# Edge tiles of a graph layer: one three-column product in place of two two-column ones, and one weighting op in place of two

## What is computed

```python
xn = layernorm(x)
Wh = xn @ W_w + W_b
e = (Wh @ a_w[:256])[dst] + (Wh @ a_w[256:])[src] + a_b      # one number per edge
e = where(e > 0, e, 0.2 * e)
ex = exp(e - segment_max(e, src)[src])
gnn = relu(segment_sum(ex[:, None] * Wh[dst], src) / segment_sum(ex, src))
x = x + gnn + linear_attention(xn)                           # 8 heads
x = x + moe(layernorm(x))                                    # 8 experts, top 2, gelu
```

## Time and profile before

| | |
|---|---|
| median of the runs | 2009.92 us (2008.76 to 2011.73) |
| span of the profiled execution, first to last instruction | 2207.5 us |
| instructions in it | 40303 |
| TensorE, matmuls | 78% busy, 13588 |
| VectorE | 76% busy, 4220 |
| ScalarE | 44% busy |
| GpSimd | 45% busy |
| mean granted TensorE clock | 0.895 |

### The profile page before, as it was taken

How to read it: one execution, slowest core, us unless ns; L and a number is a source line. 1 busy time by engine, 2 the same in 40 slices (tenths; PEclk the granted TensorE clock), 3 DMA queues, 4 the chain that set the end, 5 groups by cost and what they waited for, 6 DMA issues and landing times.

```text
span 2207.5 us, 40303 instructions
## 1 busy us (share of the span) xinstructions
PE 1718.1 (78%) x13588; PEld 1259.6 (57%) x13588; DVE 1669.8 (76%) x4220; ACT 976.2 (44%) x2300; POOL 994.8 (45%) x988
## 2 busy tenths in 40 slices
PE   3778785574785688888757888887888888889998
PEld 2557573463674466666535555555555555566666
DVE  5998998663566677776767887888888888886665
ACT  6322221121332233222235656666666656575655
POOL 3000003425566655655666666666666666640000
PEclk7898997796898788888968999999999999999999
DMA  5011111124554444333333333333333333860000
GB/s 174 16 59 52 51 66 32 42 84 115 145 165 130 118 120 119 102 94 90 90 90 87 86 90 83 94 83 94 82 95 92 86 92 83 89 56 11 11 20 13
DMA packets 121460, 182.21 MB, mean 83 GB/s; under 512 B 21490, under 2 KB 91902, under 8 KB 121214
## 3 DMA queue, kind: packets, MB, share of 16 engines
q0 software_dynamic: 45312, 120.06, 23.3%
q1 hardware_dynamic: 75904, 59.25, 8.6%
HBM read 152.43 MB, written 26.63 MB: 81 GB/s over the span
## 4 chain that ended last, share of the span: by engine, by line
DVE 42%; PE 23%; issue 16%; another core or an unknown queue 10%; ACT 4%; DVEq 2%; POOL 1%; DMA 0%; SPq 0%; ACTq 0%; POOLq 0%
PE bank L1255 6%; PE bank L1271 5%; DVE mloc L1615 4%; DVE big L1518 4%; DVE scr L1637 3%; DVE big L1523 3%; DVE work L1809 3%; DVE big L1520 2%; DVE big L1525 2%; DVE big L1796 2%; DVE scr L1483 2%; DVE work L1593 2%; DVE work L1610 2%; PE bank L947 1%
## 5 line engine op out<-in xcount | busy, mean ns | idle before, releaser
L664 POOL DMA_INDIRECT work<-table,tiles x904 | 921.0, 1019 | 546.6 <-PE bank L1142 277.8
L1271 PE MATMUL bank<-big 128*128 128x256 f16 x2352 | 327.7, 278 | 34.8 <-issue 34.5
L1255 PE MATMUL bank<-scr,big 128*128 128x512 f16 (+1 forms) x1248 | 282.3, 377 | 0.3 <-ACT big L871 0.3
L1140 PE MATMUL bank<-work,scr 128*128 128x257 f16 x904 | 269.9, 299 | 13.0 <-issue 10.5
L1271 PEld LDWEIGHTS bank<-big 128*128 128x128 f16 x2352 | 232.3, 99 | 78.3 <-issue 46.0
L1141 PE MATMUL bank<-work,scr 128*128 128x256 f16 x904 | 270.8, 300 | 5.9 <-issue 5.6
L1142 PE MATMUL bank<-work,scr 128*128 128x257 f16 x904 | 268.9, 297 | 5.9 <-issue 5.9
L1637 DVE SCALAR_TENSOR_TENSOR scr<-scr,gg,bank 128x257 f32<-128x257 f32 x452 | 216.7, 479 | 29.7 <-remote 16.6
L999 PE MATMUL bank<-big 128*128 128x208 f16 x1568 | 176.9, 269 | 67.7 <-DVE big L1525 60.9
L799 ACT ACTIVATE work<-bank 128x1024 f16<-128x1024 f16 x113 | 115.5, 1022 | 242.7 <-DVE mloc L1615 144.0
L999 PEld LDWEIGHTS bank<-big 128*128 128x128 f16 x1568 | 150.7, 102 | 94.6 <-issue 88.9
(11 more groups left out here) (340 smaller groups left out, 3494.1 us busy)
## 6 DMA issues: line engine op xcount, KB each, us to landing
work<-table,tiles POOLq DMA_INDIRECT x904
scr<-normed_cols SPq DMA_DIRECT2D x98, 128.0 KB
table<-big SPq DMA_DIRECT2D x49, 129.0 KB, 2.1
normed_rows<-scr SPq DMA_DIRECT2D x49, 128.5 KB, 2.6
big<-normed_rows SPq DMA_DIRECT2D x49, 128.5 KB
normed_cols<-big SPq DMA_DIRECT2D x49, 128.0 KB, 1.7
xs<-in_x_dram SPq DMA_DIRECT2D x4, 1536.0 KB, 14.2
out_dram<-work SPq DMA_DIRECT2D x48, 128.0 KB
```

What stands on the lines that cost most here:

```text
L664: pool.indirect_dma_start(G[:, r, j, :], None, table, bass.IndirectOffsetOnAxis(ap=col[:, t:t + 1], axis=0)).then_inc(rows_in[r // GS], 16)
L1140: pe.matmul(of[:, 0:D + 1], hi, Gh[:, r, j, 0:D + 1], start=(j == 0), stop=False)
L1255: mm = pe.matmul(bank[5 + f][:, 0:n * P], w1p[pw][:, e, h, f * P:(f + 1) * P], x2p[b % 2][px][:, h, 0:n * P], start=(h + m == 0), stop=(h ...
L1271: mm = pe.matmul(of, hTp[ph][:, k % 2, f, (j + c) * P:(j + c + 1) * P], w2p[pw][:, e, f, :], start=False, stop=(f == 1 and m == 2))
```

## The change

It does four things:

1. `prA` and `prB` become one tile `rowp` with four float16 columns per group: row value, its rest, maximum, and one unused column. `spread` makes one product of three columns per tile into a PSUM tile with three columns, where it made two of two columns.
2. `edge_scores` gets a new first op: a sum over the first two of the three columns (`tensor_reduce` from PSUM into the new tile `s0`), with a hand-over to the op that was the first.
3. `w4h` and `w4l` become halves of one tile, and one `tensor_tensor` of 2048 elements writes both weighted one-hots; it waits for `w4l`.
4. `frg` has `coff` subtracted once ahead of the loop, so that the op for `cc` adds two tensors and needs no pointer scalar. The memset of `prB` (L1560) goes.

```diff
-        prA = tiles[:, place_t:place_t + NG + 1].bitcast(F16).rearrange("p (g c) -> p g c", c=2)
-        prB = tiles[:, place_t + NG + 1:place_t + 2 * NG + 2].bitcast(F16).rearrange("p (g c) -> p g c", c=2)
+        rowp = tiles[:, place_t:place_t + 2 * NG + 2].bitcast(F16).rearrange("p (g c) -> p g c", c=4)
...
-        Shi = [piece(NC // 2, P, 2, dt=F16) for _ in range(2)]
-        Slo = [piece(NC // 2, P, 2, dt=F16) for _ in range(2)]
+        S = [piece(2, NC // 2, P, 2, dt=F16) for _ in range(2)]
...
-        w4h = sb("w4h", [P, ST], F16)
-        w4l = sb("w4l", [P, ST], F16)
+        w4p = sb("w4p", [P, 2 * ST], F16)
+        w4h, w4l = (w4p[:, k * ST:(k + 1) * ST] for k in range(2))
...
-            return bank[2][:, 0:2 * ST].rearrange("p (j c) -> p j c", c=2)
+            return bank[2][:, 0:3 * ST].rearrange("p (j c) -> p j c", c=3)
...
-                    of = spread_of(s)[:, j, :]
-                    pe.matmul(of, OT[:, j, :], prA[:, g + 1, :], start=True, stop=False)
-                    mm = pe.matmul(of, OT[:, j, :], prB[:, g + 1, :], start=False, stop=True)
+                    mm = pe.matmul(spread_of(s)[:, j, :], OT[:, j, :], rowp[:, g + 1, 0:3], start=True, stop=True)
...
-            link(dve.memset(prB[:, :, :], 0.0))
-            link(dve.memset(prA[:, 0:1, :], 0.0))
+            link(dve.memset(rowp[:, 0:1, :], 0.0))
...
-            dve.tensor_tensor(prB[:, 1:NG + 1, 0], frg, prA[:, 1:NG + 1, 0], ALU.subtract).then_inc(fr_parts, 1)
+            dve.tensor_tensor(rowp[:, 1:NG + 1, 1], frg, rowp[:, 1:NG + 1, 0], ALU.subtract).then_inc(fr_parts, 1)
+            dve.wait_ge(fr_parts, 1)
+            link(dve.tensor_scalar(frg, frg, coff[:, :], None, ALU.subtract))
...
+                dve.tensor_reduce(s0[:, :], spread_of(s)[:, :, 0:2], AX.X, ALU.add).then_inc(e_s0, 1)
+                dve.wait_ge(e_s0, s + 1)
                 dve.tensor_tensor(s1[:, :].rearrange("p (r j) -> p r j", r=GS),
-                                  spread_of(s)[:, :, 0].rearrange("p (r j) -> p r j", r=GS),
+                                  s0[:, :].rearrange("p (r j) -> p r j", r=GS),
                                   G[:, r:r + GS, :, D + 1], ALU.add).then_inc(e_s1, 1)
...
-                dve.tensor_tensor(s3[:, :], s2[:, :], spread_of(s)[:, :, 1], ALU.subtract).then_inc(e_s3, 1)
+                dve.tensor_tensor(s3[:, :], s2[:, :], spread_of(s)[:, :, 2], ALU.subtract).then_inc(e_s3, 1)
...
-                dve.tensor_tensor(w4l[:, :], w4[:, :], w4h[:, :], ALU.subtract).then_inc(e_w4l, 1)
+                dve.tensor_tensor(w4l, w4[:, :], w4h, ALU.subtract).then_inc(e_w4l, 1)
                 if s > 1:
                     dve.wait_ge(e_A, GS * (s - 1))
-                dve.tensor_tensor(Shi[s % 2], hot[s % 2], pairs(w4h[:, :], P, 1), ALU.mult)
                 dve.wait_ge(e_w4l, s + 1)
-                dve.tensor_tensor(Slo[s % 2], hot[s % 2], pairs(w4l[:, :], P, 1), ALU.mult).then_inc(e_S, 1)
+                a = w4p[:, :].rearrange("p (i r u) -> p i r u", r=1, u=2).to_broadcast([P, NC, P, 2])
+                dve.tensor_tensor(S[s % 2].rearrange("p k i r u -> p (k i) r u"),
+                                  hot[s % 2].rearrange("p (k i) r u -> p k (i r u)", k=1).to_broadcast([P, 2, NC * P]),
+                                  a, ALU.mult).then_inc(e_S, 1)
...
-                dve.scalar_tensor_tensor(cc[:, :], mx[:, k, 1:GS + 1], coff[:, :], frg[:, g:g + GS], ALU.subtract, ALU.add
-                                         ).then_inc(e_cc, 1)
+                dve.tensor_tensor(cc[:, :], mx[:, k, 1:GS + 1], frg[:, g:g + GS], ALU.add).then_inc(e_cc, 1)
```

More of the change, by code:

```diff
@@ L333, in graph_layer @@
         gg = sb("gg", [P, 4, GS])
+        s0 = sb("s0", [P, ST])
         s1 = sb("s1", [P, ST])
@@ L349, in graph_layer @@
         bank = [ctx.enter_context(nc.psum_tensor(f"bank{n}", [P, 512], F32)) for n in range(8)]
-        loaded = {n: sem("loaded_" + n) for n in ("edges", "neighbours", "x", "raw", "weights", "experts0", "experts1", "b2", "list")}
+        loaded = {n: sem("loaded_" + n) for n in ("edges", "neighbours", "raw", "weights", "experts0", "experts1", "b2", "list")}
         filled, padded = sem("filled"), sem("padded")
@@ L382, in graph_layer @@
         rows_in = [sem(f"rows_in{i}") for i in range(GR // GS)]
-        (e_fdp, e_hot, e_V, e_VT, e_ml, e_mx, e_cc, e_R, e_dR, e_gg, e_OT, e_EX, e_s1, e_s2,
+        (e_fdp, e_hot, e_V, e_VT, e_ml, e_mx, e_cc, e_R, e_dR, e_gg, e_OT, e_EX, e_s0, e_s1, e_s2,
          e_s3, e_w4, e_w4l, e_S, e_A, e_U) = (sem("e_" + k) for k in (
-             "fdp", "hot", "V", "VT", "ml", "mx", "cc", "R", "dR", "gg", "OT", "EX", "s1", "s2",
+             "fdp", "hot", "V", "VT", "ml", "mx", "cc", "R", "dR", "gg", "OT", "EX", "s0", "s1", "s2",
              "s3", "w4", "w4l", "S", "A", "U"))
@@ L771, in _ @@
             act.activation(frg, bank[0][:, 0:NG], ACT.Identity, bias=abb[:, :])
-            act.activation(prA[:, 1:NG + 1, 0], bank[0][:, 0:NG], ACT.Identity, bias=abb[:, :]).then_inc(meta_sb, 1)
+            act.activation(rowp[:, 1:NG + 1, 0], bank[0][:, 0:NG], ACT.Identity, bias=abb[:, :]).then_inc(meta_sb, 1)
             for p in range(FIRST_EARLY, EARLY):
@@ L782, in exps @@
                 act.activation(w4[:, :], s3[:, :], ACT.Exp)
-                act.activation(w4h[:, :], s3[:, :], ACT.Exp).then_inc(e_w4, 1)
+                act.activation(w4h, s3[:, :], ACT.Exp).then_inc(e_w4, 1)
             def values(s):
@@ L1138, in total @@
                     n = g % GS * GT + j
-                    hi, lo = (S[s % 2][:, n // 2, :, n % 2] for S in (Shi, Slo))
+                    hi, lo = (S[s % 2][:, k, n // 2, :, n % 2] for k in range(2))
                     pe.matmul(of[:, 0:D + 1], hi, Gh[:, r, j, 0:D + 1], start=(j == 0), stop=False)
@@ L1620, in shifts @@
                 dve.wait_ge(e_mx, s + 1)
-                dve.scalar_tensor_tensor(cc[:, :], mx[:, k, 1:GS + 1], coff[:, :], frg[:, g:g + GS], ALU.subtract, ALU.add
-                                         ).then_inc(e_cc, 1)
+                dve.tensor_tensor(cc[:, :], mx[:, k, 1:GS + 1], frg[:, g:g + GS], ALU.add).then_inc(e_cc, 1)
                 dve.wait_ge(e_cc, s + 1)
-                dve.scalar_tensor_tensor(prA[:, g + 1:g + GS + 1, 1], cc[:, :], ALPHA, cc[:, :], ALU.mult, ALU.max
+                dve.scalar_tensor_tensor(rowp[:, g + 1:g + GS + 1, 2], cc[:, :], ALPHA, cc[:, :], ALU.mult, ALU.max
                                          ).then_inc(e_R, 1)
@@ L1628, in shifts @@
                     dve.wait_ge(e_gg, s - 1)
-                dve.tensor_tensor(dR[:, s % 2, :], prA[:, g:g + GS, 1], prA[:, g + 1:g + GS + 1, 1], ALU.subtract
+                dve.tensor_tensor(dR[:, s % 2, :], rowp[:, g:g + GS, 2], rowp[:, g + 1:g + GS + 1, 2], ALU.subtract
                                   ).then_inc(e_dR, 1)
```

## The result

The changed kernel takes 2026.38 us (2024.89 to 2027.71) against 2009.34 us: the ratio is 1.0085, with a 95% interval of 1.0071 to 1.0099, so 17 us slower (14 to 20). Forecast were +10.1 us and 2020.0.

The account below looks back on a forecast made before the run. VectorE was taken to set most steps of the loop's second half, the first half only in part. Terms 14.0 + 4.4 - 3.9 - 4.4 gave +10.1 us, so 2009.9 became 2020.0 us; the 8-in-10 range was 1997 to 2036.

Parts of the forecast that it names:

- The sign and its cause: Whole loop: slower by 10.1 us, as VectorE sets most steps of the second half; chance of slower 0.56.
- s0: VectorE's new sum ahead of L1582: 0.165 us plus 0.035 hand-over, 0.20 a step, +14.0 us.
- 70 of 113 steps: L1582's pieces in the chain of waits, taken as the steps that pay for the new sum; the other 43 hide it.
- The weighting op: Single op of 2048 elements on VectorE: 1.33 to 1.34 us against 1.28, +0.055 a step, x 80, +4.4 us.
- w4l must be done first (0.20 as above): Ahead of the single weighting op: it starts 0.20 us after the w4l op, the next op 1.13 later.
- cc: VectorE's op without pointer scalar: 225 ns become 0.16 to 0.17 us, -0.055 a step, x 71, -3.9 us.
- TensorE: Spread products: 8 of 16 go, third column free, -0.2 us a step in 22 steps of the chain, -4.4 us.
- The span: Profiled 2207.5 us, to become 2217.6; runs supposed to lack many unnamed waits, terms carried over unscaled to 2009.9 us.
- (a): Loop: the added work is hidden, GpSimd's gathers set the first half's pace; 2014 us or less, to 2006; chance 0.20.
- (b): TensorE's instruction fetch: 7.4 packets fewer save 16 to 36 us; at 3 us each, 1998 us; chance 0.24.
- (c): Single weighting op loses its two-at-a-time rate, 2.29 us instead of 1.22, +86 us, 2108 us; chance 0.04.

Follow-up runs that it names:

- the second sum: The changed kernel with the sum s0 made twice, the second time after a wait for the first: 2047.80 us, ratio 1.0180.
- the doubled add: The kernel before with L1582, the first op of edge_scores, and its hand-over made twice: 2031.87 us, ratio 1.0098.
- the new profile: The kernel before, unchanged, measured and profiled once more: 2008.89 us, ratio 0.9997, profiled span 2010.5 us.
- the two parts alone: The kernel before with only the three-column product and the sum s0 (parts 1 and 2): 2021.44 us, ratio 1.0059.
- the waits in the better order: The kernel before with only the single weighting op (part 3), waiting for e_w4l first and then e_A: 2019.87 us, ratio 1.0042.
- half of the products: The kernel before without the second (prB) spread product of each tile: 2009.36 us, ratio 0.9987.
- part 4 and two ops: The changed kernel with the two weighting ops of the kernel before (parts 1, 2 and 4): 2019.96 us, ratio 1.0039.
- part 3 alone: The kernel before with only the single weighting op of 2048 elements that waits for w4l: 2023.35 us, ratio 1.0066.

## Why the prediction was right, and what was off

**The sign and its cause** held: VectorE sets most steps, and it got more to do. The op added to the kernel before without anything else cost 0.89 of its full price, and the second sum in the changed kernel about 0.8. TensorE's shorter stream, which the change buys with it, is worth 2.6 us alone.

**s0.** Price as forecast (0.201 a step). What was counted at nothing, L1582 behind the sum, costs 0.014 more. The number that I multiplied with, 70 of 113 steps (0.62), was too low: the doubled add shows about 0.89. The disturbed profile isn't to blame for that. Counted in the same way, the new profile of the same kernel has L1582 in the chain 60 times, L1598 72, L1621 61, and the spread products 560 times, which is 35 steps. By these counts the sum would have been 12.0 + 4.0 - 3.4 - 7.0 = +5.6 us, farther from the measured value. The count itself is the weak term: the chain names one path in a step, and where two paths end within tenths of a microsecond, the one that it leaves out costs nearly as much. That the first profile had 70 and not 60 was luck. For the two parts alone the terms (14.0 - 4.4) say +9.6, measured are +11.9 (9 to 14).

**The weighting op** is the step that failed: "w4l must be done first (0.20 as above)". The duration and the distance to the next op (1.143 against 1.13) were right, the start after w4l was 0.263. There are two waits ahead of the op, and I had priced a hand-over by a row with one. +4.4 us was forecast, +13.3 is what it costs alone and 9 to 11 beside the others. With the waits in the better order it is +8.4. The rule of the Trainium skill, VectorE: DVE Perf Modes, section "The DRAIN you can't avoid", taken as the prediction took it (no op starts before the pipe is empty), would have made this part a gain of 2 us. The starts (1.143 us after an op of 1.226) and the time contradict that. The section itself adds that a next op that is not held starts earlier, and the trace agrees with this sentence.

**cc.** The op fell by 0.06 as forecast, -3.9 us. Alone it gave nothing measurable (-2 to +2), beside the others 4.6, give or take 4. The size of this term is not shown.

**TensorE.** -4.4 forecast, -2.6 [-4.4, -0.8] measured for half of the products. The 0.2 us a step and the third column at no cost were right (0.390 to 0.189 us). With the measured starts in place of mine and the old counts, the sum would have been 70 x 0.215 + 80 x 0.123 - 71 x 0.058 - 2.6 = 15.1 + 9.8 - 4.1 - 2.6 = +18.2 us. The measured 17 to 19 is there; the mis-sized wait is most of the gap to +10.1. That this sum fits so well is in part chance, since its counts were too low (0.62 to 0.71, measured 0.7 to 0.9).

**The span.** I supposed that runs without a profiler lack the unnamed waits. They do; but so does every other profiled run. The terms had to be carried over unscaled, as they were.

**Rivals.** (a), hidden: in part. The first 60 steps pay 0.08 of 0.280 us, not nothing, and what hides the rest is in part another wait than the one for the gathers (below). The second half swallows little. (b), the shorter stream: 7 packets fewer were counted rightly, the worth of one was not 2 or 3 us but 0.4 at the most likely, if anything at all. Its argument that several engines stand still together in the unnamed waits was misread: in the 62 waits of L1582 of over 0.3 us, 130 us in all, TensorE was busy for 84. (c), the lost rate (its own numbers add up to 2106, not 2108): 1226 ns for 2048 elements excludes it; here the trace agrees with the Trainium skill, Vector Engine (DVE) Microarchitecture Reference, section 5.1, that a row read twice keeps the rate.

**Where a part comes back.** By the price of the doubled ops (0.8 to 0.9 of 113), VectorE's 0.280 us a step would cost 25 to 28 us, and the change costs 17 to 19. The same gap is in the two other kernels with the three-column product and s0: parts 1 and 2 alone would be 0.215 x 113 x 0.85 = 21 and are 12; with part 4 and two ops, 0.157 x 113 x 0.85 = 15 and 8. So something gives 7 to 10 us back, and halving the products of the kernel before gives 2.6. The traces show the place. In 21 of the first 60 steps of the kernel before, VectorE stands ahead of L1598 and waits for ScalarE's exponentials. The same step (35) in the kernel before, with half the products, with the add made twice, and with parts 1 and 2:

```profile
908.57 0.17 DVE L1598 TENSOR_TENSOR w4l<-w,w4h 128x8 f16<-128x8 f32 x1 [1.37 <-ACT w4h L783]
...
901.76 0.17 DVE L1597 TENSOR_TENSOR w4l<-w,w4h 128x8 f16<-128x8 f32 x1 [1.17 <-ACT w4h L783]
...
912.40 0.17 DVE L1599 TENSOR_TENSOR w4l<-w,w4h 128x8 f16<-128x8 f32 x1 [1.17 <-ACT w4h L783]
...
907.27 0.17 DVE L1597 TENSOR_TENSOR w4l<-w,w4h 128x8 f16<-128x8 f32 x1 [0.95 <-ACT w4h L783]
```

The exponentials are late here because ScalarE first does two ops on a product of the attention (in the kernel before):

```profile
907.26 0.60 ACT L819 ACTIVATE scr<-bank 128x512 f32<-128x512 f32 x1 [1.37 <-PE bank L1175]
```

TensorE comes to L1175 straight from the spread products, with no pause between them. So in such a step the spread lies on the path that ends last, and L1582 lies beside it: an op more on VectorE is hidden (the wait is 0.20 shorter), 0.20 us less on TensorE is gained, and with both the wait is 0.42 shorter. Over the whole profile this wait is 40.4 us in the kernel before, 37.7 with half the products, 38.2 with the add made twice, and 40.2 with part 3 alone; with parts 1 and 2 it is 30.4, with part 4 and two ops 34.5, and 31.3 and 31.7 in the two profiles of the changed kernel. These last four profiles, all with the three-column product, have 6 to 10 us less of it than the kernel before, which is the size of the gap.

**What stays open.** The steps with that wait explain some 21 x 0.2 = 4 us by TensorE's shorter row (an estimate from the step above). The rest of the 6 to 10 us lies in single waits of 2 to 4 us, which are up to 1.7 us longer in one kernel than in another for a reason that the traces don't name, and each kernel has one or two profiles. A second hint is that *shortening* the kernel before brings little either way (cc: 0, products: 2.6), while lengthening costs nearly in full. In the second half of its loop GpSimd has little room. Its busy time in the new profile (columns: us, POOL busy, clock, DMA share, GB/s) and its waits between 1110 and 1780 us:

```profile
1110.00:1780.00 670.00, 487.30 (x454) 0.97 0.46 97
```
```profile
POOL work L664 <- issue: 124.6, 409, 0.3
POOL work L664 <- PE bank L1142: 40.2, 45, 3.4
```

Only 40 of 670 us are waits for a free place in the ring; the rest is gathers and their issue. With the add made twice it is

```profile
POOL work L664 <- PE bank L1142: 91.7, 76, 5.0
```

and 74 in the changed kernel. A kernel that hands ring places back sooner has at most those 40 us to win before the gathers set the pace, in part or in full in single steps. That would explain why shortening pays less than lengthening; it is argued from these waits, and no run took gathers away or made them quicker, so it isn't shown.

## What to carry to other kernels

Price an edit by the distance between starts in a timeline, not by durations, and look for a row with the same hand-over: as many waits, and the last one to come true in the same place. Merging two ops isn't a gain when the first of them didn't have to wait for what the merged one must wait for. Before waits are read from a profile, check that its span is near the median of the runs; here it was 10% off, and VectorE's durations were good and the waits were not. How often a line stands in the chain is no price: 60 of 113 in the sound profile, where an added op cost 0.89 of 113. What an op costs is told by doubling it.

## What was not expected of the hardware

- Two waits ahead of one VectorE op: when the one written second comes true last, the op starts 0.263 us after the op it depends on; written first, 0.194. The op itself was 0.16 us in both. The steps without the other wait had 0.19 to 0.24.
- A `tensor_tensor` on 8 float32 numbers takes 173 ns with both operands in SBUF, and 158 with one in PSUM (L1582 after and before). About half of that is its place: where the add is made twice, both from PSUM, the first takes 158 ns and the second, right behind the op that it waits for, 167; the sum made twice takes 167 and 174. That leaves some 6 ns for the operand, and PSUM isn't the dearer side here.
- One profiled execution of the same kernel had a span of 2207.5 us, another 2010.5, with equal durations on VectorE (L1603 had 684 ns in both) and longer ones on TensorE (L1140: 299 ns against 285).
- 904 matmuls of two columns and their weight loads less, with seven packets of instructions: 2.6 us.
